# One x tile, loads and fills inside the layer norms, an unrolled last stage, and three band transfers begun by ScalarE

## What is computed

```python
x = x + attn0(layernorm(x))          # 16 heads of 8, softmax over all 512 tokens
x = x + stack(layernorm(x))          # 6 layers: local attention + gated feed-forward
x = x + attn1(layernorm(x))          # as attn0, with rotary positions
y = layernorm(x)                     # gated mix of each token with the one before
yk = mu_k * y + (1 - mu_k) * previous(y)
yr = mu_r * y + (1 - mu_r) * previous(y)
out = x + sigmoid(yr @ Wr.T) * (relu(yk @ Wk.T) ** 2 @ Wv.T)
```

## Time and profile before

| | us |
|---|---|
| median of 3 runs | 4958.59 |
| lowest and highest | 4957.13, 4967.54 |
| the profiled execution | 4963.93 |
| its span (first to last instruction) | 4962.1 |

### The profile page before, as it was taken

One profiled execution on the slowest core, in us unless ns is written; L12 is line 12 of the kernel. 1 busy time (PEld: TensorE's weight loads), 2 busy tenths in 40 slices (PEclk: granted clock), 3 DMA queues, 4 the chain that ended last, 5 costly groups with the idle time before them and its releaser, 6 DMA issues. The chain is left out here.

```text
span 4962.1 us, 116892 instructions
## 1 busy us (share of the span) xinstructions
PE 4540.5 (92%) x46384; PEld 2667.8 (54%) x46384; DVE 3541.4 (71%) x3746; ACT 2295.9 (46%) x3418; POOL 2443.8 (49%) x3467
## 2 busy tenths in 40 slices
PE   5999869999999999999999999999999995588896
PEld 2233346666666666666666666666666663222223
DVE  4777467787777777777777777877777784477763
ACT  0566534444444444444444444444444442055564
POOL 1111056665666666666566666666666661221210
PEclk7999979999999999999999999999999997589997
DMA  2322032222222222222222222222222221122210
GB/s 52 62 54 61 3 98 55 59 60 64 69 63 53 57 73 68 55 59 63 72 57 63 54 69 69 59 53 59 63 63 57 60 59 47 34 53 53 52 28 19
DMA packets 181061, 281.67 MB, mean 57 GB/s; under 512 B 58032, under 2 KB 79792, under 8 KB 174896
## 3 DMA queue, kind: packets, MB, share of 16 engines
q1 hardware_dynamic: 180880, 279.24, 23.7%
HBM read 61.70 MB, written 17.56 MB: 16 GB/s over the span
## 5 line engine op out<-in xcount | busy, mean ns | idle before, releaser
L958 DVE SCALAR_TENSOR_TENSOR l_t<-l_r,l_qkvec,l_tab 128x1024 f32<-128x1024 f32 x768 | 933.3, 1274 | 31.4 <-ACT l_sq L871 28.9
L477 DVE TENSOR_REDUCE a_nmax<-a_pair 128x2 f32<-128x1024 f32 x512 | 609.4, 1220 | 262.7 <-PE a_pair L559 262.5
L395 ACT ACTIVATE a_pt<-a_st 128x512 f32<-128x512 f32 x1024 | 541.8, 604 | 284.8 <-PE a_st L543 279.5
L909 ACT ACTIVATE l_p<-l_p 128x1024 f32<-128x1024 f32 x192 | 203.1, 1058 | 644.8 <-DVE l_p L1015 644.8
L805 POOL TENSOR_TENSOR l_ntmp<-l_seed 128x32 f32<-128x32 f32 (+1 forms) x480 | 110.7, 231 | 788.5 <-ACT l_seed L860 769.4
L832 POOL TENSOR_TENSOR l_u<-l_t 128x512 f32<-128x512 f32 x384 | 491.0, 1279 | 0.0
L833 POOL TENSOR_TENSOR l_u<-l_t 128x512 f32<-128x512 f32 x384 | 490.6, 1277 | 0.0
L1207 PE MATMUL l_r<-l_pbd,l_va 128*64 128x160 f32 (+1 forms) x6144 | 444.3, 298 | 48.0 <-DMA l_pbd<-l_pt 48.0
L838 POOL TENSOR_TENSOR l_p<-l_p,l_srec 128x1024 f32<-128x1024 f32 x192 | 365.1, 1901 | 221.4 <-DVE l_srec L1036 183.3
L1117 PE MATMUL l_r<-xs,l_wqkv 128*128 (+1 forms) x768 | 430.4, 672 | 42.1 <-DVEq L935 23.4
L1207 PEld LDWEIGHTS l_r<-l_pbd,l_va 128*64 128x64 f32 x6144 | 398.5, 138 | 110.0 <-issue 110.0
(11 more groups left out here) (184 smaller groups left out, 7562.7 us busy)
## 6 DMA issues: line engine op xcount, KB each, us to landing
l_kbd<-l_kn SPq DMA_DIRECT2D x1536, 64.0 KB, 2.0
l_pbd<-l_pt SPq DMA_DIRECT2D x1344, 64.0 KB, 2.0
a_ks<-a_scr SPq DMA_DIRECT2D x96, 192.0 KB
a_qs<-a_scr SPq DMA_DIRECT2D x288, 64.0 KB
a_scr<-a_parts SPq DMA_DIRECT2D x48, 256.0 KB, 2.5
l_pbd<-l_pt SPq DMA_DIRECT2D x192, 56.0 KB, 2.0
l_wqkv<-in_wqkv SPq DMA_DIRECT2D x6, 1536.0 KB, 7.4
l_wo<-in_wo SPq DMA_DIRECT2D x6, 512.0 KB, 3.9
```

Of the source, the lines that this page charges most:

```text
L395: nc.scalar.activation(pt[n % 2][:, r, :], st[(4 * n + r + par) % 3][:], ACT.Exp, scale=SC).then_inc(exp_done, 1)
L477: nc.vector.tensor_reduce(out=nmax[:, n, 2 * i:2 * i + 2], in_=pair[i][:], op=ALU.max, axis=AX.X, negate=True).then_inc(pair_dve[i], 1)
L958: last = nc.vector.scalar_tensor_tensor(out=t[a][:, 2 * half:2 * half + 2, :], in0=R[a][:, half, :].unsqueeze(1).to_broadcast([D, 2, T]), ...
```

## The change

- **x.** One SBUF tile `x` from start to end instead of `x_first` and `x_second`. In the stack, whose SBUF is full, its two halves serve as the temporaries `t`; so `x` is still copied to DRAM and fetched. The copy is begun inside `b_ln`, the fetch in the stack's last pass.
- **Layer norms.** `layernorm_pass` takes `loads` for SP and `fills` for POOL: each stage's transfers and fills are issued in its layer norm's block. All fills go to POOL. The input comes in four pieces of two sequences, and the mean products wait for their piece. The stack's result is added inside `a1_ln` (`added`), two sequences ahead of the subtraction. A layer norm has no semaphore set of its own; the stage's set holds its semaphores. The blocks `load`, `keep`, `fetch`, `zero_before`, `add_stack` and `zero_first` are gone.
- **Last stage.** No loop. POOL scales the shifted tokens (TENSOR_SCALAR) instead of ACT; DVE mixes sequence b, squares b - 1 and finishes b - 2 in turn; the result has a tile of its own for each sequence.
- **Band.** The three transfers of L780 move from SP to ACT. ACT waits for a semaphore of DVE's transposition and issues them behind `expand` and ahead of `copy_v` for c = 0 to 2, and ahead of both for c = 3.

```diff
-def layernorm_pass(nc, name, C, src, dst_parts):
+def layernorm_pass(nc, name, C, sem, src, xc, sq, dst_parts, arrived=None, added=None, loads=None, fills=None):
...
+        if loads is not None:
+            @block.sync
+            def _(sp):
+                loads(sp)
+
+        if fills is not None:
+            @block.gpsimd
+            def _(pool):
+                fills(pool)
...
+                if arrived is not None:
+                    pe.wait_ge(arrived[b], 16)
+                if added is not None:
+                    pe.wait_ge(added_ready, b + 1)
...
+            def add(b):
+                if added is not None and b < NB:
+                    for part, y in added(b):
+                        last = nc.vector.tensor_tensor(src[part, b, :], src[part, b, :], y, ALU.add)
+                    v.drain().then_inc(added_ready, 1)
+
+            add(0)
+            add(1)
             for b in range(NB):
+                add(b + 2)
                 v.wait_ge(mean_ready, b + 1)
...
+        def fills(pool):
+            done = Tally()
+            for i in range(2):
+                nc.gpsimd.memset(ks[i][64:ROWS], 1.0).then_inc(filled, 1)
+                pool.wait_ge(filled, done.next(filled))
+                nc.gpsimd.memset(vt[i][:], 0.0).then_inc(filled, 1)
+                pool.wait_ge(filled, done.next(filled))
+                nc.gpsimd.memset(vt[i][:, :, :, HD:HD + 1], 1.0).then_inc(filled, 1)
+                pool.wait_ge(filled, done.next(filled))
...
-        t = [sb(f"t{a}", [D, 4, T]) for a in range(2)]
+        t = [x[:, 4 * a:4 * a + 4, :] for a in range(2)]
...
-                        for w in range(1, 4):
-                            q, above = slice(32 * w, 32 * w + 32), slice(32 * w - 32, 32 * w)
-                            sp.dma_start(band[above, w, :], turned[q, 0].rearrange("p u i -> p (u i)")).then_inc(pbd_full[c % 2], 16)
...
+                    if b is None and c == 0:
+                        sp.dma_start(x[:], x_kept).then_inc(S["fetched"], 16)
...
+                    def place_upper_band():
+
+                        act.wait_ge(S["pt_ready_act"], seen.next(S["pt_ready_act"]))
+                        for w in range(1, 4):
+                            q, above = slice(32 * w, 32 * w + 32), slice(32 * w - 32, 32 * w)
+                            act.dma_start(pbd[c % 2][above, w, :],
+                                          pt[c % 2][q, 0].rearrange("p u i -> p (u i)")).then_inc(pbd_full[c % 2], 16)
+
+                    if c == 3 and live(c, 3, b, prev):
+                        place_upper_band()
                     if c == 3 and b is not None:
                         copy_v()
                     if has_ss:
                         expand()
+                    if c < 3 and live(c, 3, b, prev):
+                        place_upper_band()
                     if c < 3 and b is not None:
                         copy_v()
...
-            with act.Fori(0, NB // 2) as i:
-                for p in range(2):
-                    for a in range(2):
-                        last = nc.scalar.activation(prev[p][a][:], xn[:, 2 * i + p, 0:T], ACT.Copy, scale=comu[:, a:a + 1])
-                    last.then_inc(prev_ready, 1)
...
+        @block.gpsimd
+        def _(pool):
+            for b in range(NB):
+                if b >= 2:
+                    pool.wait_ge(mix_ready, b - 1)
+                for a in range(2):
+                    last = nc.gpsimd.tensor_scalar(prev[b % 2][a][:], xn[:, b, 0:T], comu[:, a:a + 1], None, ALU.mult)
+                last.then_inc(prev_ready, 1)
...
+            for b in range(NB + 2):
+                if b < NB:
+                    mixtures(b)
+                if 1 <= b <= NB:
+                    squared_relu(b - 1)
+                if b >= 2:
+                    result(b - 2)
```

323 lines of the change are left out of this document (148 added, 175 removed).

## The result

| | before | after |
|---|---|---|
| median us (runs) | 4957.86 (4) | 4838.99 (4) |
| lowest and highest | 4939.74, 4967.54 | 4828.0, 4846.12 |
| profiled execution | 4963.9 | 4843.5 |

The changed kernel takes 0.9755 of the time of before (95% interval 0.9736 to 0.9775), 118.9 us less by the medians. The forecast was 4845, in a range of 4812 to 4893.

What follows compares the result with a forecast made beforehand. PE was taken to bound the stack, no engine the stage boundaries, a dependence chain the last stage. Boundaries and last stage 70.0 plus stack 44 gave 114 us off 4963.9: 4850 profiled, 4845 median, range 4812 to 4893.

Steps and rivals of the forecast that it cites:

- Rival 3: Layer norms: b_ln at half clock loses 6 to 9 us, another rising wins 6 to 10; inside the forecast's 0.80.
- start: Kernel start: PE's first product waits for 512 KB of x, not 2 MB; gain 4.2 us (2 to 5).
- first attention: Weights there before L639 gain 3.9 us, fills moved from beside DVE's cast 5.1; sum 9.0 (7 to 10).
- front of the stack: Between b_ln and the stack: copy, loads and fills move beside b_ln, leaving 0.4 us; gain 21.3 (19 to 22).
- behind the stack: From stack's end to the norm's first subtraction: fetch in the last pass, additions in the norm; gain 18.6 us (17 to 20).
- second attention: PE's 6.22 us in front of L639 shrink to 1.2; gain 5.0, nothing more from the cast.
- last stage: After the last norm: mixtures start earlier, a sequence takes 4.5 us, POOL's scaling 0.65; gain 14.2 us (4 to 20).
- band: Stack, L1207's waits for band transfers: 48 us less 6 remaining, less 7 for DVE's scaling of q; gain 35.
- clock in the stack: Seven fewer half-clock pieces in the stack's iterations, 1.3 us each; gain 9 us (-10 to 25).
- Rival 4: Last stage: POOL and DVE lock each other out, 5.0 us a sequence, gain 10, total 4849; inside the forecast's 0.80.
- rival 2: Stack: ACT becomes the bound; at d us per issue, 10d - 7 us an iteration, 4989 at d = 1.0; chance 0.04.
- Rival 1: Stack: ACT's band transfers land late and waits stay; stack gains 9 instead of 44, median 4880; chance 0.16.

Runs made afterwards that it cites:

- e13: The changed kernel once more, unaltered, with a second profile: 4844.51 us (6 runs), ratio 0.9773 to the kernel before.
- e7: The changed kernel, but POOL fills a_ks at the start of the attention's own block, as before the change: 4883.05 us in one run.
- e4: The changed kernel with each of ACT's three band transfers split in two, six issues for each chunk: 4967.28 us in one run.

## Why the prediction was right, point by point

The total came within 6 us. The parts didn't: the stack was forecast 18 to 21 us too high, the boundaries 10 too low. That these errors partly cancel is luck: the measured parts below come to 104 to 106 us, where 114 were forecast and the medians give 114 and 119 (*Rival 3*). The size of each part, forecast and measured (before against `e13`, in which a0_ln has the clock it had before):

| term | forecast | measured |
|---|---|---|
| start | 4.2 | 4.3 |
| first attention | 9.0 | 3.3 + 7.0 = 10.3 |
| front of the stack | 21.3 | 21.0 |
| behind the stack | 18.6 | 18.9 |
| second attention | 5.0 | 4.2 + 3.7 = 7.9 |
| last stage | 14.2 | 18.0 |
| semaphores | -2.3 | inside the others |
| boundaries and last stage | 70.0 | 80.4 |
| band | 35 | 14, by plain iterations |
| clock in the stack | 9 | 9 to 12 is left of 23 to 26; 7 to 9 by its half-clock time |

- *Start, front, behind the stack*: right by their own steps. Loads and fills did lie beside the norm, and in front of the stack 0.77 us was left where 0.4 was forecast. Behind the stack the forecast 18.6 was for the first subtraction; by that milestone it is 18.0, and the 18.9 of the table is for the first mean.
- *First attention*: right in mechanism; `e7` shows the fill blocking the cast, two of them even. The 1.9 us more than the 5.1 are clock: the two products at the earlier trace rows, 2.08 and 1.91 us for a pair, take 1.10 and 1.02. Before, PE had been idle for 5 us and the granted clock was half from 50.66; now they stand behind 1 us of idle time and the clock is full.
- *Second attention*: "its first cast came after the fills, so no more" was right for the fills. The 3.7 us that came on top are the same clock effect, on the four products of L647 too (3.78 to 1.98): granted half from 4255.88 to 4269.53 before, full from 4164.26 to 4177.91 now.
- *Last stage*: the direction was right, both prices wrong, and they partly cancelled. POOL's scaling was priced at 0.65 from a one-input instruction of 512 elements; it takes 1.56 by itself and 1.82 on average. That row is a cast to bf16 on 8 partitions, without a scalar operand; which of these makes the difference no run separates. So the first mixture came 3.5 us after the norm's end and not 1.8. On the other side a sequence took 3.8 us, not 4.5: PE ran at full clock nearly throughout (0.91, was 0.75) instead of being half way to its low clock. Rival 4 is there in a mild form: mixtures 25% longer beside POOL and POOL's scaling up to 47% longer beside DVE, neither blocked for a whole instruction: a mixture that starts 0.05 us behind a scaling ends 0.34 us before it. The Trainium skill (SBUF — State Buffer, Who interferes with whom) has a DVE instruction with two inputs in SBUF contend with a GpSimd one that reads; the trace agrees: the mixtures grow from 0.75 to 0.93, and beside the squares and sums it is POOL that grows, from 1.56 to 2.30, while they keep 0.684 and 0.692.
- *Band*: the sum was 48 - 6 - 7. The first two are right: 42 forecast, 0.86 x 48 = 41 measured in c = 0 to c = 1. The step that failed is "I charge 34 x 0.2 = 7" for DVE's scaling of q behind it. It costs 0.53 in each iteration, 25 us. The row showed 65 such waits with 0.29 each, and the charge took the listed wait for the delay and counted the 34 chunks of the band wait at less than that; the slack of DVE against a PE that comes 0.9 earlier was not worked out from the timeline, where of the 0.87 us by which PE came earlier, only 0.34 fitted.
- *Clock*: "I take 7 fewer", of pieces at half clock, was wrong in form. There are 53 in before, 55 and 53 in the two profiles after, but 232 us in all before and 215 and 218 after. They moved, from c = 0 to c = 1 into c = 2 to c = 3. The 9 us agree in size only.
- *ACT's slack*: the issues cost 0.6 each as assumed, but begin with the expansion's start, so for c < 3 the slack was larger by 1.0 than in the account of rival 2, and 10d - 7 is too high (`e4`: 2.5 us an iteration at twice the issues, not 5.0). Rival 1 fell: the transfers of both engines did not queue up, 34 us of the band waits went. The Trainium skill (DMA: Bandwidth & Descriptors, Issuing engines are not separate DMA queues) has a second issuing engine save only the issuing time; that is what was saved here, 1.8 us of a queue of 4.9, and it was enough to end most of the waits (48.0 us in 34 before, 13.5 in 8 after).
- *Rival 3* came true upward in the first profile (a0_ln 11 us shorter) and not in the second. The boundaries' 10 us too little and the stack's 20 too much would by themselves put the median near 4855. It lies 10 to 16 us lower. The profiled execution of `e13`, from which the parts are measured, is the slowest of its six and 14.5 us above their median, that of before 5.3 above its own; what the quicker executions did otherwise was not profiled, so that it was the clock is not shown.

## What to carry to other kernels

When a wait is taken off one engine, follow the next chunk row by row and work out which chain between engines becomes the shortest in slack; a listed wait behind the one removed is a lower bound, since breaking a row of matmuls costs more than the idle time shown. Loads and fills that stand between stages can be priced from the timeline to about half a microsecond, and are the safer part of such a change. The price of an instruction on another engine has to come from a row with the same operands: here a cast and a scaling with as many elements per partition differed by a factor of 2.6 to 3.
